# First batch of a four-batch block kernel: norm by halves with statistics on VectorE, conv as multiply-adds on VectorE, adding DMAs from the second batch on

## What is computed

```python
x = L0_attn_x                                    # (4, 1024, 128)
x = x + _layernorm(_L0_attn_ref(_layernorm(x), Wqkv, Wo, conv_w))
x = x + _layernorm(_L0_ffn_ref(_layernorm(x), ...))
# inside _L0_attn_ref, per batch (8 heads of 16 channels):
qkv = x @ Wqkv
q, k, v = jnp.split(qkv, 3, axis=-1)
# tele: softmax over the keys at offsets 0, 1, 2, 4 ... 512 back, times v at those offsets
# conv: 7-tap depthwise causal conv of v along the tokens
vpad = jnp.pad(v, ((0, 0), (KCONV - 1, 0), (0, 0)))
conv = conv_general_dilated(vpad, conv_w, feature_group_count=c)
# low: linear attention with elu features (fq, fk), summed over all tokens
h = tele + conv_h + low
return x + h @ Wo
```

## Time and profile before

| | |
|---|---|
| time, median of 3 runs (lowest to highest) | 318.48 us (316.63 to 319.97) |
| the profiled execution: its time, and its span | 320.01 us, 318.0 us |
| TensorE busy, of the span | 256.4 us (81%) |
| VectorE busy | 234.7 us (74%) |
| ScalarE busy | 205.7 us (65%) |
| GpSimd busy | 90.1 us (28%) |
| mean granted TensorE clock | 0.894 of 2.4 GHz |
| DMA moved | 34.46 MB, of it 12.58 MB on the software queue (adding DMAs) |

### The profile page before, as it was taken

One profiled execution on the slowest core, in us unless ns is written; L12 is line 12 of the kernel. 1 busy time (PEld: TensorE's weight loads), 2 busy tenths in 40 slices (PEclk: granted clock), 3 DMA queues, 4 the chain that ended last, 5 costly groups with the idle time before them and its releaser, 6 DMA issues.

```text
span 318.0 us, 4568 instructions
## 1 busy us (share of the span) xinstructions
PE 256.4 (81%) x1527; PEld 173.4 (55%) x1527; DVE 234.7 (74%) x567; ACT 205.7 (65%) x471; POOL 90.1 (28%) x153
## 2 busy tenths in 40 slices
PE   6664977089579779997897799989798899888894
PEld 6323443087345437766553448658445296774283
DVE  5049936298996669889988699399976897936842
ACT  1578655047737974699869963798488615375851
POOL 3912150101514310304566002125741103131013
PEclk9785797789959989999999969999799589799998
DMA  7300999900789940121989830106889601000003
GB/s 215 94 0 16 220 225 227 226 7 0 159 235 240 200 82 3 33 67 25 224 240 205 195 68 0 34 2 136 241 231 227 117 2 33 0 3 0 1 2 99
DMA packets 23809, 34.46 MB, mean 108 GB/s; under 512 B 3989, under 2 KB 17134, under 8 KB 23786
## 3 DMA queue, kind: packets, MB, share of 16 engines
q1 hardware_dynamic: 20330, 21.59, 24.2%
q0 software_dynamic: 3456, 12.58, 21.5%
HBM read 5.07 MB, written 2.10 MB: 23 GB/s over the span
## 4 chain that ended last, share of the span: by engine, by line
PE 43%; ACT 29%; SPq 8%; DVE 7%; POOL 6%; issue 3%; DMA 3%; POOLq 0%; DVEq 0%; ACTq 0%
PE psH L1215 9%; PE psA L1135 6%; PE psY L1312 5%; PE psF L1276 5%; ACT xn L633 4%; SPq L341 3%; POOL rstd L427 3%; SPq L344 3%; ACT xn L539 3%; ACT squares L626 2%; PE psY L1164 2%; PE psA L1127 2%; PE psY L1226 2%; PE psF L1255 2%; DMA v_shift<-v_tok 2%
## 5 line engine op out<-in xcount | busy, mean ns | idle before, releaser
L264 DVE TENSOR_TENSOR prods<-qT,kT 128x1024 f32<-128x1024 f32 (+1 forms) x44 | 48.8, 1166 | 13.6 <-ACT qT L527 13.6
L425 POOL TENSOR_SCALAR var<-ss 128x4 f32<-128x4 f32 (+1 forms) x25 | 11.1, 443 | 123.1 <-ACT squares L679 62.1
L1215 PE MATMUL psH<-ident,prods 128*128 128x128 f32 x324 | 43.1, 285 | 0.0
L1215 PEld LDWEIGHTS psH<-ident,prods 128*128 128x128 f32 x324 | 39.3, 149 | 2.3 <-issue 2.3
L427 POOL TENSOR_TENSOR rstd<-var,neg_half 128x4 f32<-128x4 f32 (+2 forms) x29 | 37.2, 1283 | 2.4
L902 DVE TENSOR_TENSOR prods<-v_shift,prob 128x896 f32<-128x896 f32 x32 | 35.8, 1119 | 0.0
L1276 PE MATMUL psF<-x3T,w 128*128 128x512 f32 x58 | 31.7, 661 | 0.1
L1016 DVE TENSOR_TENSOR hid<-hid,psG 128x512 f32<-128x512 f32 x32 | 20.8, 684 | 14.9 <-PE psG L1298 14.3
L1135 PE MATMUL psA<-xnT,wqkv 128*128 128x512 f32 x48 | 30.0, 771 | 2.1 <-ACT xnT L527 2.1
L1183 PE MATMUL psA<-prods,slot_sel 128*32 128x512 f32 x168 | 25.3, 656 | 4.4 <-DVE prods L264 3.0
L439 POOL DMA_DIRECT2D convT<-tapT x12 | 10.9, 907 | 60.8 <-DMA convT<-tapT 29.4
(11 more groups left out here) (199 smaller groups left out, 557.1 us busy)
## 6 DMA issues: line engine op xcount, KB each, us to landing
v_shift<-v_tok SPq DMA_DIRECT2D x20, 448.0 KB
convT<-tapT POOLq DMA_DIRECT2D x12, 512.0 KB, 4.6
x_in<-L_attn_x SPq DMA_DIRECT2D x4, 512.0 KB, 3.6
x_res<-L_attn_x SPq DMA_DIRECT2D x4, 512.0 KB, 9.2
tapT<-xnT POOLq DMA_DIRECT2D x4, 512.0 KB, 9.9
convT<-kexp POOLq DMA_DIRECT2D x4, 512.0 KB, 7.5
tapT<-qexp POOLq DMA_DIRECT2D x4, 512.0 KB, 9.7
out<-y_out SPq DMA_DIRECT2D x7, 256.0 KB, 2.3
```

The costliest lines, as they stand in the source:

```text
L264: return eng.tensor_tensor(prods[:, QUADS * (s % 2) + q, t0:T], qT[:, t0:T], kT[:, PRE - off + t0:PRE - off + T], ALU.mult)
L1215: ins = pe.matmul(dst, terms[:, j % TERM_BUFS, m, :], ident[:], is_transpose=True, start=False, stop=(m == live[-1]))
```

## The change

For batch 0 alone: (1) the statistics, the variance and the mean times rstd are done by halves of four tiles, all on VectorE but for the power, which stays on GpSimd (`first_rstds`); (2) VectorE, not ScalarE, evacuates the turned x; (3) ScalarE no longer scales the seven taps and GpSimd no longer issues the six adding DMAs; VectorE does the conv into `convT[0]`, one multiply and six multiply-adds (`first_conv`), four of these ahead of `softmax_logits(0)` and three behind it; (4) waits and counts of the semaphores concerned start with batch 1, so `features(1)` and `evacuate_x(1)` no longer wait for an adding DMA. From batch 1 on everything is as before.

```diff
+            def first_rstds():
+                for half in range(2):
+                    cols = slice(half * TPH, (half + 1) * TPH)
+                    pool.wait_ge(first_var, half + 1)
+                    nc.gpsimd.tensor_tensor(rstd1[:, cols], var1[:, cols], neg_half[:, cols],
+                                            ALU.pow).then_inc(first_rstd, 1)
...
-            ln1(0)
+            first_rstds()
             constants()
             more_constants()
-            sum_taps_first(0)
...
-                if attn:
+                if attn and b:
                     sum_taps_second(b)
                 if more:
                     ln1(b + 1)
                 if ffn and attn:
                     ln3(u1)
-                if attn:
+                if attn and b:
                     sum_taps_third(b)
...
             def normalise1(b, tiles=range(NT)):
-                act.wait_ge(ln1_ready, upto(b, 1, 1))
                 if b:
+                    act.wait_ge(ln1_ready, upto(b - 1, 1, 1))
                     act.wait_ge(xn_kept, upto(b - 1, 1, 1))
                 for j in tiles:
+                    if b == 0 and j % TPH == 0:
+                        act.wait_ge(first_normed, j // TPH + 1)
...
             def features(b):
                 act.wait_ge(psA_free, freed(b - 1, PSA_Q, 1))
-                act.wait_ge(sums_added, N_DMA * upto(b, N_SUMS, 0))
+                if b >= 2:
+                    act.wait_ge(sums_added, N_DMA * upto(b - 1, N_SUMS, 0))
...
             normalise1(0)
-            evacuate_x(0)
+            act.wait_ge(psA_free, freed(-1, PSA_X, 1))
             evacuate_k(0)
             evacuate_q(0)
             features(0)
             evacuate_v(0)
-            scale_taps(0, range(0, 4))
...
-                    scale_taps(b, range(5 if b else 4, TAPS))
+                    if b:
+                        scale_taps(b, range(5, TAPS))
...
+            def first_norm():
+
+                dve.wait_ge(x_in_ld, N_DMA)
+                first_chain.start(dve, 0)
+                for half in range(2):
+                    tiles = range(half * TPH, (half + 1) * TPH)
+                    cols = slice(half * TPH, (half + 1) * TPH)
+                    for j in tiles:
+                        last = nc.vector.bn_stats(bn[:, j, :], x_in[:, j, :])
+                    first_chain(last)
+                    for j in tiles:
+                        last = nc.vector.bn_aggr(mv[:, j, :], bn[:, j, :])
+                    first_chain(last)
+                    nc.vector.tensor_scalar(var1[:, cols], mv[:, cols, 1], EPS, None, ALU.add).then_inc(first_var, 1)
+                for half in range(2):
+                    cols = slice(half * TPH, (half + 1) * TPH)
+                    dve.wait_ge(first_rstd, half + 1)
+                    nc.vector.scalar_tensor_tensor(out=nmr1[:, cols], in0=mv[:, cols, 0], scalar=-1.0,
+                                                   in1=rstd1[:, cols], op0=ALU.mult,
+                                                   op1=ALU.mult).then_inc(first_normed, 1)
+                nc.vector.tensor_scalar(neg_mean[:, 0, :], mv[:, :, 0], -1.0, None, ALU.mult)
+                for half in range(2):
+                    dve.wait_ge(psA_full, filled(-1, PSA_X, half))
+                    nc.vector.tensor_copy(xnT[:, bass.ts(half, HALF)], psA[:, half, :]).then_inc(psA_free, 1)
...
+            def first_conv(shifts):
+
+                if 0 in shifts:
+                    dve.wait_ge(psA_free, freed(-1, PSA_V, 1))
+                    dve.wait_ge(conv_ld, N_DMA)
+                    conv_chain.start(dve, 0)
+                for shift in shifts:
+                    v, w = vT[:, VPRE - shift:VPRE - shift + T], cw[:, TAPS - 1 - shift:TAPS - shift]
+                    if shift == 0:
+                        conv_chain(nc.vector.tensor_scalar(convT[0][:], v, w, None, ALU.mult))
+                    else:
+                        conv_chain(nc.vector.scalar_tensor_tensor(out=convT[0][:], in0=v, scalar=w, in1=convT[0][:],
+                                                                  op0=ALU.mult, op1=ALU.add))
...
-            stats(0)
+            first_norm()
...
+                    if b == 0:
+                        first_conv(range(0, 4))
                     softmax_logits(b)
+                    if b == 0:
+                        first_conv(range(4, TAPS))
```

More of the change, by code:

```diff
@@ L63 @@
 N_SOFTMAX_STEPS = 5
+N_FIRST_STEPS = 4
 N_SUMS, N_SIDE = 4, 2
+N_CONV_STEPS = TAPS
 N_FRONT = 3
@@ L228, in block_kernel @@
         bn_done = sem("bn_done")
+        first_step, first_var = sem("first_step"), sem("first_var")
+        first_rstd, first_normed = sem("first_rstd"), sem("first_normed")
         ln1_ready, ln2_ready, ln3_ready, ln4_ready = sem("ln1_ready"), sem("ln2_ready"), sem("ln3_ready"), sem("ln4_ready")
@@ L251, in block_kernel @@
         softmax_chain = Chain(softmax_step, N_SOFTMAX_STEPS)
+        first_chain = Chain(first_step, N_FIRST_STEPS)
+        conv_chain = Chain(conv_step, N_CONV_STEPS)
         def bank(tile):
@@ L446, in sum_taps_second @@
             def sum_taps_second(b):
[L447 to L448 removed]
+                pool.wait_ge(tap_scaled, upto(b - 1, TAPS, 6))
+                pool.wait_ge(sums_added, N_DMA * upto(b - 1, N_SUMS, 1))
                 add_tap(b, 0, 4, sums_added)
[L450 removed]
+                pool.wait_ge(side_added, N_DMA * upto(b - 1, N_SIDE, 1))
                 add_tap(b, 2, 5, side_added)
             def sum_taps_third(b):
[L454 to L455 removed]
+                pool.wait_ge(tap_scaled, upto(b - 1, TAPS, 7))
+                pool.wait_ge(sums_added, N_DMA * upto(b - 1, N_SUMS, 2))
                 add_tap(b, 0, 6, sums_added)
[L457 to L458 removed]
+                pool.wait_ge(sums_added, N_DMA * upto(b - 1, N_SUMS, 3))
+                pool.wait_ge(side_added, N_DMA * upto(b - 1, N_SIDE, 2))
                 add_tap(b, 0, 2, sums_added)
@@ L913, in weigh @@
                 beside(2)
+            def first_conv(shifts):
[7 more added lines that the diff above has]
+                        conv_chain(nc.vector.tensor_scalar(convT[0][:], v, w, None, ALU.mult))
+                    else:
+                        conv_chain(nc.vector.scalar_tensor_tensor(out=convT[0][:], in0=v, scalar=w, in1=convT[0][:],
+                                                                  op0=ALU.mult, op1=ALU.add))
             def add_conv(b, half):
                 dve.wait_ge(terms_summed, upto(b, NT, TPH * (half + 1)))
-                dve.wait_ge(sums_added, N_DMA * upto(b, N_SUMS, N_SUMS))
+                if b:
+                    dve.wait_ge(sums_added, N_DMA * upto(b - 1, N_SUMS, N_SUMS))
                 cols = bass.ts(half, HALF)
```

29 lines of the change are left out of this document (11 added, 18 removed).

## The result

| | before | after |
|---|---|---|
| time, median (lowest to highest) of 4 runs | 318.24 us (316.63 to 319.97) | 310.03 us (308.98 to 310.72) |
| the profiled execution: time, span | 320.01, 318.0 us | 310.14, 308.4 us |
| VectorE busy | 234.7 us (74%) | 245.3 us (80%) |
| mean granted TensorE clock | 0.894 | 0.926 |

The ratio of after to before is 0.974 with a 95% interval of 0.968 to 0.980.

What follows compares the result with a forecast made beforehand. Batch 0's first `weigh` was bound by the shifts' DMA chain, then by VectorE's own chain. Moving it from 61.62 to 54.0 gains 7.6 us; 318.48 - 7.6 = 310.9, rounded to 311.0, range 308.0 to 314.3.

Steps and rivals of the forecast that it cites:

- What bounds the kernel: Batch 0 up to first `weigh`: DMA traffic of shifts and adding DMAs until 61.6, afterwards VectorE's own chain.
- tap 0: VectorE's first conv instruction, one input and a scalar: 1.1 us taken, with 0.7 as the skill page's estimate.
- the clock in the middle: TensorE between 26 and 37, waiting for products: a clock fall at the second head sum, 0.7 us given back.
- The front end's clock: TensorE up to `qT`: 18.3 if the clock falls, 15.4 if it never does; 3.5 us earlier taken between them.
- clock falls in the middle: Rival, second head sum to turn at 1.2 GHz: `zden` about 2.5 us later, gain 4.8, 313.7 us; chance 0.17.
- clock full throughout the front end and no fall later: Rival, TensorE in batch 0: first `weigh` at 52.05, gain 9.6, 308.9 us; chance 0.17.
- `zden` following tap 3 with no idle time: Sign of being right, VectorE in batch 0: `zden` starts straight after the fourth conv instruction, zero idle time.
- GpSimd beside the products: `ln1(1)` near 26 beside VectorE's products: GpSimd stretches, while 44 products never took more than 1.227 us.
- The rule: Rival, products beside `ln1(1)`: two-SBUF-input VectorE and SBUF-reading GpSimd instructions exclude each other; up to 1.9 us, 312.8; chance 0.03.
- Behind it: After first `weigh`: `features(1)` no longer waits; the stretch 61.6 to 78 and later batches move as a block.
- the rivals that end at 316 and 322.5 us: Gain given back in batches 1 to 3, 316, chance 0.05; TensorE staying at 1.2 GHz in `weigh`, 322.5, chance 0.01.
- the rival by which SP's issuing sets their pace: Batch 0's shifts don't get faster without adding DMAs: landing at 54.6, gain 7.0, 311.5 us; chance 0.04.

Runs made afterwards that it cites:

- experiment 1: The kernel before with the new front end alone, ScalarE's seven taps and the six adding DMAs kept; 314.18 us, ratio 0.984.
- experiment 2: The kernel before with batch 0's conv on VectorE alone, the front end left old; 312.77 us, ratio 0.978.
- experiment 5: The changed kernel once more, same code, in a later comparison on another chip; 306.84 us, ratio 0.958.
- experiment 4: The changed kernel with 32 more identity transposes on TensorE ahead of batch 0's second head sum; 310.69 us, ratio 0.972.
- experiment 7: The changed kernel with batch 0's taps 4 to 6 scaled by ScalarE and summed by three adding DMAs after the shifts land; 302.75 us, ratio 0.948.
- experiment 3: The kernel before with ScalarE evacuating `v_tok` and `fk_tok` of batch 0 first, scaling all seven taps afterwards; 312.54 us, ratio 0.979.
- experiment 9: The kernel of experiment 7 without the wait for the shifts, so its adding DMAs run beside them; 304.26 us, ratio 0.954.

## Why the prediction was right

**What bounds the kernel.** Right. The traffic set the pace of the shift issues: with the adding DMAs they took 26.3 us at the old front end and 26.8 at the new one, without them 13.5 at both (experiments 1 and 2). VectorE's own chain was the next bound, and the first `weigh` at 53.9 was forecast for 54.0.

**The terms**, each against what the trace of after shows:

| term | forecast | measured |
|---|---|---|
| `xn` starts | 7.5 | 7.43 |
| `qT` ready and first product earlier by | 3.5 | 4.46 |
| first four products | 4.63 | 5.09 |
| `v_tok` evacuated | 23.3 | 22.4 |
| 18 shift issues | at most 17.2 | 13.5 |
| tap 0 | 1.1 | 0.73 |
| three multiply-adds | 3.75 | 3.92 |
| idle ahead of `zden` (the clock in the middle) | 0.7 | 1.27 |
| from the end of the logits to `den`, more than before | 2.85 | 2.96 |
| first `weigh` | 54.0 | 53.89 |

Five terms were mis-sized or missed, and they nearly cancel: 0.96 and 0.37 us better against 0.46, 0.17 and 0.57 worse, which leaves 0.1 better. (The prediction ends tap 3 at 44.36; its own terms give 44.31, which changes nothing.)

That 54.0 met 53.89, and 311.0 met 310.03, is therefore in part luck. In the first comparison the gain was 8.2 us, of which batch 0 gives 7.9. In experiment 5 the same code had a median of 306.84 us, below the range of 308.0 to 314.3, and a gain of 13.5 us, of which batch 0 gives 8.7 in the profiled executions. The mechanism up to `weigh` is shown; the time of the whole program was not forecast to better than the 5 us by which the later batches move it.

*The front end's clock.* The forecast lay between a fall (`qT` at 18.3) and none (15.4). The windows of after show none:

```profile
8.80:11.10 2.30, 1.06 (x8) 0.85 (x9) 0.69 (x1) 1.82 (x5) 2.17 (x11) 1.00 0.46 134
11.10:15.70 4.60, 4.60 (x13) 1.48 (x10) 0.69 (x1) 2.39 (x4) 4.46 (x27) 1.00 0.48 116
```

The granted clock is 1.00, 2.4 GHz, where it was 0.59 and 0.52 before. TensorE was busy for 1.06 us of the first stretch and for all of the second, where it had been idle throughout the first before. The first product, which waits for `qT`, started between 15.6 and 15.9 in all nine profiles with the new front end, and between 19.6 and 20.3 in the three with the old one. With nine of nine on one side, "no fall" should have been the forecast, not a value between the two; the 3.5 was chosen between two values from rows and had no row of its own.

*The clock in the middle* differs between executions. The rival "clock falls in the middle" happened in the profiled execution of after, and not in the fifth experiment's, with the same code. The second head sum ran at half the clock and `zden` waited 1.27. The term of 0.7 lies between the two outcomes, 1.27 and nothing, and comes from no row; with a wait in two of nine profiles it was too large on average. The rival put `zden` 2.5 later. The turn of the scores did come late, at 39.81 against 37.27 in experiment 5, but the conv, which ends at 40.1, covered half of that. Experiment 5 shows the other rival, "clock full throughout the front end and no fall later", in all that counts: `weigh` at 52.45 against the 52.05 forecast for it. The prediction's signs disagree here, too: its sum has the 0.7, while its list has `zden` following tap 3 with no idle time.

*GpSimd beside the products* was missed. I had looked at `ln1(1)`, which the change moved beside later instructions of VectorE; there the power took 1.64 us, `nmr` 0.60, and the seven products beside and behind it 7.50. The prediction argued from 44 products that had never taken more than 1.227 us that GpSimd is the one that stretches; but none of those had a select beside it. The rule was right, in a small form, at an instruction that the rival did not name. The collision happened with `gate_sel`, which the change does not touch: the products came 4.5 us earlier and met it. What was overlooked came from looking only at instructions that the diff moves, not at those that stand still while the engine beside them comes early.

*Tap 0* took 0.73, below the 1.1 that I took between two rows. The Trainium skill's "VectorE: DVE Perf Modes" led to an estimate of 0.7 for one input and a scalar on fp32 in SBUF, and the trace agrees.

**Behind it.** Right. `features(1)` starts at 50.96 with no wait, and ScalarE waits at the squares instead, where it costs nothing:

```profile
50.96 1.06 ACT L603 ACTIVATE kexp<-kT 128x1024 f32<-128x1024 f32 x1
...
65.39 0.31 ACT L636 ACTIVATE squares<-yc 128x128 f32<-128x128 f32 x1 [10.33 <-DVE yc L981]
```

The 7.75 us of `weigh` are 7.86 at the mark of batch 1 and 7.9 at those of batches 2 and 3. Nothing was given back. TensorE's granted clock was 0.56 from 55.2 to 58.6 and 1.00 from 58.6 to 70.4, much as before, so it did not stay cold behind `weigh`. So the rivals that end at 316 and 322.5 us did not occur. The issues' 13.5 us rule out the rival by which SP's issuing sets their pace. The 1.7 us of the tail weren't forecast. The twelve profiled executions, whose code behind the mark of batch 1 is the same, took 230.8 to 236.4 us from there to the end. From the mark of batch 3 on, before took 100.9 us at a granted clock of 0.90 and after 99.2 at 0.94; experiment 4, a changed kernel, took 100.9 at 0.90 as well, so the long form is not bound to the old code. But there is only one profile of before, which had 236.3 from the mark of batch 1, and experiment 5's gain is larger than batch 0 explains. That the change leaves the later batches alone on average is not shown.

## What to carry to other kernels

When an engine waits for a transfer and the DMA share is near 1, ask whose bytes fill the queues: here six adding DMAs that nobody needed yet doubled the time in which the transfers on the path could be issued, from 13.5 to 26.3 us. Bytes that must be moved anyway can go behind the urgent ones (experiment 7), and work can be put where an engine waits in any case. Where its chain has become the bound, added work costs its full length less the wait it fills: the three taps behind the logits took 3.92 us and filled 0.91. When a chain is started earlier, go through what the other engines do in its new place, untouched instructions too, and when an order is changed follow each in-order engine past the wait that you removed (experiment 3).

## What the runs showed of the hardware

- A VectorE product of 128x1024 with two SBUF inputs took 1.68 us instead of 1.23 beside GpSimd's select of 24x512 bf16, and the select 1.47 instead of 0.66. The product `nmr` of 128x8 on GpSimd took 0.60 beside other products in after and 0.20 in experiment 3 where VectorE was idle; those seven products took 7.50 us in both.
- One multiply of 128x1024 fp32 by a value for each partition took 0.73 us, a multiply-add on the same shape 1.28, and 1.30 from one to the next where each waits for the last.
- Adding DMAs of 512 KB between SBUF tensors landed 4.5 us after their issue with nothing beside them (experiment 7), 7.0 and 8.2 us beside the shifts (experiment 9), and up to 12.7 us in experiment 3. The issue of one shift on SP's queue took 0.55 to 0.98 us without them in after; with them it stretched to 3.1 us in experiment 1 and 3.6 in experiment 3.
- TensorE's clock in the middle of batch 0 fell at the first head sum or at the second in different executions of one kernel (after and experiment 5). The changed kernel's ratio to before was 0.974 in one comparison and 0.958 in another, and the intervals (0.968 to 0.980, 0.953 to 0.962) do not overlap; why stays open.
